# First cross attention of a decoder: weighing products from two rounded parts of probabilities and values

## The reference, cut to what matters

```
kv = concat([norm(ctx), norm(x)], axis=tokens)      # 8 x 256 x 128
q  = norm(x) @ Wq + bq ;  k, v = split(kv @ Wkv + bkv)
p  = softmax(q k^T / sqrt(128))                     # 8 sequences x 8 heads x 128 x 256
y  = (p v) @ Wo + bo
x  = layernorm(x + y)
```

## Time and profile before

| | us |
|---|---|
| median of 3 runs (lowest to highest) | 960.88 (958.42 to 967.42) |
| the profiled execution: device time | 967.44 |
| the profiled execution: span from first to last instruction | 965.6 |
| the stage's loop, from the first turn to the end of the last weigh | 51.0 to 123.1 of the span |

### The profile page before, as it was taken

How to read it: one execution, slowest core, us unless ns; L and a number is a source line. 1 busy time by engine, 2 the same in 40 slices (tenths; PEclk the granted TensorE clock), 3 DMA queues, 4 the chain that set the end, 5 groups by cost and what they waited for, 6 DMA issues and landing times.

```text
span 965.6 us, 15347 instructions
## 1 busy us (share of the span) xinstructions
PE 895.5 (93%) x5222; PEld 575.4 (60%) x5222; DVE 675.1 (70%) x1123; ACT 556.8 (58%) x963; POOL 182.2 (19%) x157
## 2 busy tenths in 40 slices
PE   8999998999799888889899988999899999999997
PEld 4566645665535543345545544776246887778885
DVE  4667626877768758668858845542547998899996
ACT  5356624555555446366656541332476888888886
POOL 0111021432000000000020007332300433334430
PEclk9999999999999998999999999999999999999999
DMA  9000000111000000000000061402106999999992
GB/s 358 3 1 0 0 13 22 33 33 63 1 1 2 1 1 1 0 1 1 2 1 2 2 238 46 129 26 61 44 1 169 229 229 228 231 234 235 237 233 68
DMA packets 27746, 76.76 MB, mean 79 GB/s; under 512 B 4464, under 2 KB 10864, under 8 KB 27264
## 3 DMA queue, kind: packets, MB, share of 16 engines
q1 hardware_dynamic: 26448, 73.50, 29.3%
q0 software_dynamic: 1248, 2.57, 0.8%
HBM read 72.31 MB, written 5.27 MB: 80 GB/s over the span
## 4 chain that ended last, share of the span: by engine, by line
PE 54%; DVE 19%; DMA 13%; ACT 9%; issue 4%; SPq 1%; DVEq 0%; POOL 0%; ACTq 0%; POOLq 0%
DMA arena<-m_comb 12%; PE ps L743 4%; PE ps L745 4%; PE ps L1106 4%; PE ps L744 4%; PE ps L582 3%; PE ps L574 3%; DVE ps L2359 2%; PE ps L599 2%; PE ps L1122 2%; DVE parts L777 2%; PE ps L593 2%; PE ps L280 2%; PE ps L217 2%; PE ps L1385 2%
## 5 line engine op out<-in xcount | busy, mean ns | idle before, releaser
L743 PE MATMUL ps<-parts 128*128 128x512 f32 x416 | 171.0, 411 | 8.6 <-DVE parts L957 3.3
L745 PE MATMUL ps<-parts 128*128 128x512 f32 x416 | 162.8, 391 | 0.0
L744 PE MATMUL ps<-parts 128*128 128x512 f32 x416 | 162.6, 391 | 0.0
L773 ACT ACTIVATE parts<-ps 128x512 fp32r<-128x512 f32 x192 | 114.9, 599 | 61.5 <-PE ps L745 31.2
L777 DVE TENSOR_TENSOR parts<-ps,parts 128x512 fp32r<-128x512 f32 x192 | 132.3, 689 | 6.0 <-ACT parts L773 0.8
L2359 DVE TENSOR_TENSOR ps<-ps,arena 128x512 f32<-128x512 f32 x156 | 108.3, 694 | 11.1 <-DMA arena<-m_comb 10.3
L743 PEld LDWEIGHTS ps<-parts 128*128 128x128 f32 x416 | 78.4, 188 | 42.7 <-DVE parts L777 9.5
L761 POOL TENSOR_TENSOR parts<-ring,zeros 128x1024 fp32r<-128x1024 f32 (+2 forms) x36 | 50.9, 1422 | 236.7 <-PE ps L745 183.9
L1915 ACT ACTIVATE ps<-ps 128x512 f32<-128x512 f32 x156 | 90.8, 582 | 7.2 <-PE ps L745 4.6
L745 PEld LDWEIGHTS ps<-parts 128*128 128x128 f32 x416 | 78.3, 188 | 16.8
L744 PEld LDWEIGHTS ps<-parts 128*128 128x128 f32 x416 | 78.4, 188 | 15.1 <-issue 0.5
(11 more groups left out here) (447 smaller groups left out, 1415.9 us busy)
## 6 DMA issues: line engine op xcount, KB each, us to landing
arena<-m_comb SPq DMA_DIRECT2D x156, 256.0 KB, 6.4
ring<-m_in SPq DMA_DIRECT2D x20, 512.0 KB, 8.5
arena<-m_in SPq DMA_DIRECT2D x4, 1408.0 KB, 10.3
pack<-pack_in SPq DMA_DIRECT2D x1, 2058.5 KB, 10.4
ring<-m_up_in SPq DMA_DIRECT2D x8, 256.0 KB, 2.6
slots_x<-empty_in SPq DMA_DIRECT2D x1, 1491.6 KB, 7.0
pack<-pack_in SPq DMA_DIRECT2D x1, 1186.0 KB, 14.5
pack<-pack_in SPq DMA_DIRECT2D x1, 1149.5 KB, 12.1
```

Source lines behind the costliest of these rows:

```text
L743: nc.tensor.matmul(dst, w_high, x_high, start=start, stop=False, skip_group_check=True)
L744: nc.tensor.matmul(dst, w_high, x_low, start=False, stop=False, skip_group_check=True)
L745: return nc.tensor.matmul(dst, w_low, x_high, start=False, stop=stop, skip_group_check=True)
L773: nc.scalar.activation(m_hh[0:rows, p], ps[0:rows, src, :], ACT.Copy).then_inc(R(t, "_hh"), 1)
```

## The change

ScalarE no longer copies one half of the turned probabilities and VectorE the other. ScalarE now rounds both halves (two 128 x 512 activations into `x_pth`, fp32r), and VectorE makes both remainders (two 128 x 512 subtractions, bank minus `x_pth`, into `x_ptl`, fp32r), each after the ScalarE instruction of its half. GpSimd, after its copy of a sequence's rows, rounds them into `x_kvh` and subtracts into `x_kvl`. TensorE's weighing becomes six fp32r matmuls of 128 x 512 in place of two float32 ones: high x high, low x high, high x low, for the two halves. The product of the two remainders is left out. The turn of a window waits for the remainders of the window before. Buffers move so that the fp32r ones lie in the fp32r view of the arena.

```diff
-        x_kvts = A(16960, 2, 2, P)
-        x_p = A(17472, 2, 4, 2 * P)
-        x_pt = A(19520, 2, 2, 512)
+        x_p = A(23424, 2, 4, 2 * P)
+        x_kvts = A(22200, 2, 2, P)
...
+        x_kvh, x_kvl = [parts[:, lo - PARTS:lo - PARTS + 512].rearrange("p (a b c) -> p a b c", a=2, b=2) for lo in (16960, 21600)]
+        x_pth, x_ptl = [parts[:, lo - PARTS:lo - PARTS + 2048].rearrange("p (a b c) -> p a b c", a=2, b=2) for lo in (19520, 17472)]
...
             def x_turn(v, w):
                 pe.wait_ge(S("x0_pn"), 4 * (w + 1))
-                pe.wait_ge(S("x0_ptA"), w + 1)
-                pe.wait_ge(S("x0_ptB"), w + 1)
+                pe.wait_ge(S("x0_ptL"), 2 * w + 1)
...
             def x_weigh(b, v, w, slot):
                 if v == 0:
-                    pe.wait_ge(S("x0_kvts"), b + 1)
-                pe.wait_ge(S("x0_ptA"), w + 2)
-                pe.wait_ge(S("x0_ptB"), w + 2)
+                    pe.wait_ge(S("x0_kvts"), 3 * b + 3)
                 pe.wait_ge(S("x0_o"), w + 1)
+                pe.wait_ge(S("x0_ptH"), 2 * w + 2)
                 for s in range(2):
-                    ins = mm(bank(6 + v), x_kvts[:, slot, s, :], x_pt[:, v, s, :], start=(s == 0), stop=(s == 1))
+                    mm(bank(6 + v), x_kvh[:, slot, s, :], x_pth[:, v, s, :], start=(s == 0), stop=False)
+                for s in range(2):
+                    mm(bank(6 + v), x_kvl[:, slot, s, :], x_pth[:, v, s, :], start=False, stop=False)
+                for s in range(2):
+                    pe.wait_ge(S("x0_ptL"), 2 * w + 2 + s)
+                    ins = mm(bank(6 + v), x_kvh[:, slot, s, :], x_ptl[:, v, s, :], start=False, stop=(s == 1))
...
# ScalarE, x_body
                     act.wait_ge(S("x0_turned"), w + 1)
-                    A_(x_pt[:, k % 2, 0, :], bank(4), ACT.Copy).then_inc(S("x0_ptA"), 1)
+                    for s in range(2):
+                        A_(x_pth[:, k % 2, s, :], bank(4 + s), ACT.Copy).then_inc(S("x0_ptH"), 1)
...
# VectorE, x_body
-                    dve.wait_ge(S("x0_turned"), w + 1)
-                    V.tensor_copy(x_pt[:, k % 2, 1, :], bank(5)).then_inc(S("x0_ptB"), 1)
+                    for s in range(2):
+                        dve.wait_ge(S("x0_ptH"), 2 * w + 1 + s)
+                        V.tensor_tensor(x_ptl[:, k % 2, s, :], bank(4 + s), x_pth[:, k % 2, s, :], ALU.subtract).then_inc(S("x0_ptL"), 1)
...
# GpSimd, x_keys_values
                 G.tensor_copy(x_kvts[:, slot], ...).then_inc(S("x0_kvts"), 1)
+                pool.wait_ge(S("x0_kvts"), 3 * b + 1)
+                G.tensor_tensor(x_kvh[:, slot], x_kvts[:, slot], zeros[:, 0:1].unsqueeze(2).to_broadcast([P, 2, P]), ALU.add).then_inc(S("x0_kvts"), 1)
+                pool.wait_ge(S("x0_kvts"), 3 * b + 2)
+                G.tensor_tensor(x_kvl[:, slot], x_kvts[:, slot], x_kvh[:, slot], ALU.subtract).then_inc(S("x0_kvts"), 1)
```

More of the change, by code:

```diff
@@ L1784, in x_body @@
                 x_outputs(2 * i + 1, 1, 4 * i + 3)
-            for name in ("x0_ptA", "x0_o", "x0_o"):
+            for name in ("x0_o", "x0_o"):
                 credited(act, name)
@@ L2042, in x_body @@
                         x_maxima(k % 2, w + 2)
-            credited(dve, "x0_ptB")
+            credited(dve, "x0_ptL")
             x_maxima(0, 0)
```

## The result

The changed kernel takes 987.03 us (median of 4, 983.86 to 988.60), the kernel before beside it 961.12 (median of 4). The ratio is 1.0254 with a 95% interval of 1.0226 to 1.0282: slower by 25.9 us between the medians, or 24.4 us of 961 by the ratio, where 23.8 were forecast and 984.7 predicted. Each of the steps can now be read from the profile after.

The account below looks back on a forecast made before the run. The prediction took a VectorE-ScalarE ring of 4.49 us per window as the bound, not TensorE. Its terms 21.8 + 1.4 + 0.6 = 23.8 us, on the median 960.9, gave 984.7 us, range 978 to 997.

Parts of the forecast that it names:

- Bound: Stage's loop before the change: pace is a 4.49 us VectorE-ScalarE ring per window, not TensorE's need of 4.33.
- The new ring: Stage's loop: rounding and both remainders enter the ring, 6.17 us instead of 4.49; thirteen times 1.68 is 21.8 us.
- Ends of iterations: Copy of outputs(4i+3) between exps and next rounding: 0.48 us more, three times in the stretch, 1.4 us.
- Start and tail: Before the loop's first maxima nothing lost; from last maxima to residual seed 9.84 us instead of 9.22, 0.6 more.
- Nothing is lost: Start of the loop: VectorE free at 55.40 despite two subtractions, in time for the first maxima at 55.57.
- Sum: Whole kernel: 21.8 + 1.4 + 0.6 = 23.8 us slower, nothing given back after the loop.
- GpSimd: Two more instructions per sequence, 1.34 us, hidden in the loop; 8 us over 6 sequences if not.
- Hidden: GpSimd's added 1.34 us per sequence costs nothing: two windows (12 us) between sequences, rows prepared two sequences ahead.
- the extra 4 us: GpSimd instructions of 0.6 to 0.7 us blocking VectorE's multiplications once for each of 6 loop sequences; left out of sum.
- Clock: Rival: TensorE idles twice per window, clock falls to half in half the loop's windows, 12 us more, 997; chance 12%.
- the stretch at 552 us: Sign against the clock falling: from 552 to 558 us TensorE, busy 4.25 of 6 us, stayed at full clock.

Follow-up runs that it names:

- maxima first: Changed kernel reordered: VectorE takes maxima(w+2), normalise(w+1), then remainders(w); scores one window earlier, waiting for exps only: 962.26 us, ratio 0.9978.
- GpSimd apart: Changed kernel in the maxima first order, GpSimd's jobs held until multiplications end, plain copy dropped: 954.24 us, ratio 0.9927; kernel before likewise, copies kept: 959.10 us.
- one wait, no work: Kernel before with VectorE's copy of bank 5 waiting for ScalarE's copy of bank 4 instead of the turn: 982.69 us, ratio 1.0194.
- own half: Changed kernel with VectorE rounding and subtracting bank 5 right after the turn, ScalarE rounding bank 4 alone: 979.80 us, ratio 1.0198.

## Why the prediction was right

*Bound.* That the pace of the stage was a ring over VectorE and ScalarE and not the nearly full TensorE was the step on which all hung. Runs show it from outside. For the kernel before: one wait added costs 18.7 us, and with maxima first and GpSimd apart the maxima come 4.32 apart, TensorE's need, where the ring had held them at 4.49. For the changed kernel: 0.46 us taken from TensorE in each window gives nothing.

*The new ring.* 6.17 forecast, 6.18 measured, each hand-over within 0.02. The wait of the first subtraction was forecast from 1.22 to 3.70 in the ring, 2.48 us, and is 2.49.

*Ends of iterations.* 0.48 three times forecast, and 6.65 instead of 6.17 three times found.

*Start and tail.* "Nothing is lost" at the start holds for the clock time (55.51 against 55.57) but not for the stage, which began 0.48 us earlier after the change: from the maxima of window 0 to the first in the loop it is 10.48 us where it was 10.06, 0.4 lost. The forecast counted from the end of the turn, and from there it was right (3.10 us from the first rounding to the maxima, 3.11 forecast). But the turn itself was longer in this execution; before and after:

```profile
51.03 1.23 PE L1428 MATMUL ps<-pack,arena 128*128 128x128 f32 x8 [1.70 <-DVE arena L2032]
```

```profile
50.63 1.75 PE L1428 MATMUL ps<-pack,arena 128*128 128x128 f32 x8 [1.78 <-DVE arena L2037]
```

The granted clock from 51 to 52 us was 0.93 before and 0.50 after. The tail was 0.6 forecast and is 0.9: the roundings came 1.13 after the turn and not 1.07, and the first products 0.2 later than worked out.

*Sum.* 23.8 forecast. In the profile the stage is 24.6 longer (0.4 at the start, 23.3 between the maxima, 0.9 in the tail), and the ratio says 24.4. The medians say 25.9, and the difference lies within the scatter of the executions (983.9 to 988.6 after, 958.4 to 967.4 before). Part of it may be the clock: the profiled execution after was the fastest of four, with a mean granted clock of 0.985, and the others had 0.976 to 0.981. Where they lost it no trace shows.

*GpSimd.* "Hidden" was right for the changed kernel: its multiplications took 1.14 us in every window, and where the two met it was GpSimd's copy that was longer, 0.47 in place of the 0.40 it takes alone:

```profile
86.71 0.47 POOL L2407 COPY arena<-arena 128x256 f32 x1 [9.87 <-PE ps L1442]
87.26 0.61 POOL L2409 TENSOR_TENSOR parts<-arena,zeros 128x256 fp32r<-128x256 f32 x1
87.95 0.73 POOL L2411 TENSOR_TENSOR parts<-arena,parts 128x256 fp32r<-128x256 f32 x1
```

The copy starts at 86.71, at the end of the multiplications (85.78 to 86.92), and the other two run beside maxima that read PSUM. The forecast had the copy start some 5.8 us into the ring; it started at 6.04, with only the last of the four multiplications left. This was luck of phase, and the extra 4 us that the forecast's sentence on the shared port pair gave did not come. But the slowing is real in this stage: in the run with maxima first, where the same jobs began just ahead of the multiplications, these took 1.7 us longer five times and 0.9 the sixth. The Trainium skill (SBUF — State Buffer, the notes on the shared port pair) has a VectorE instruction in a two-port mode and a GpSimd one exclude each other for a whole instruction. The 1,126 ns of one multiplication that takes 350 alone fit being held up by one GpSimd instruction of 0.73; that this is the reason is argued from the durations and not shown.

*Clock.* In the profiled execution it stayed at full with TensorE busy 70% of the loop, as the stretch at 552 us had suggested. In the run with less work on TensorE it fell to a mean of 0.72 in two stretches of 6 us in the loop, and to 0.52 from 140 to 146 us, in its tail. All four of its executions had a lower mean clock (0.964 to 0.974) than any of the changed kernel (0.976 to 0.985). It also fell in the tails of two other runs, to 0.76 (one wait, no work) and 0.74 (own half) from 128 to 134 us. What parts these from the changed kernel is not settled by these runs.

## What to carry to other kernels

An instruction that fills a wait is free only as long as what releases it comes before that wait ends. So before giving it another releaser, find the engine and the place in its list on which the new one stands: here the rounding stood behind the very exps that VectorE was waiting for, and a lighter TensorE could not help. When the busiest engine's need for a round is less than the round, write the round out as a ring of waits until it adds up, then put the change into that sum; and if a change is slower by its place, reorder before giving it up: the same arithmetic (less one plain copy on GpSimd), in an order that leaves TensorE as the pace and GpSimd away from VectorE's SBUF work, was 0.7% faster than before.

## What the hardware showed that I had not expected

GpSimd's work slowed four of VectorE's SBUF multiplications from 1.14 to as much as 2.82 us, and did not touch maxima or remainders, which read PSUM: in the run with GpSimd apart they lie beside its work and take 1.22 us and, two of them, 1.28. And TensorE's clock fell inside a loop in the run that took work from it: it was 1.00 with 61.1 of 87 us busy, and 0.72 on average in two stretches of 6 us of the run that asks 0.46 us less of it for each window.
